# Expert tiles of a mixture-of-experts layer: 32x32 block transposes on VectorE placed by DMA, in place of transposes on TensorE, with the down products two tiles behind

## The chip, the cores and the metric

One core of one Trainium2 chip runs the whole program. The metric is the device time in microseconds (us) of one execution. TensorE (PE in the profile) does matmuls and transposes, VectorE (DVE), ScalarE (ACT) and GpSimd (POOL) elementwise work; SyncE (SP) and ScalarE issue the plain DMAs here, GpSimd the indirect ones.

## The reference

Four residual steps on x, 4 x 512 tokens of 512 dims: a cross-attention that yields softmax weights, a ternary Hadamard feed-forward, a grouped cross-attention with 32 heads, and a routed mixture of experts. Only the last is touched by the change:

```python
def _routed_moe(x, gate_w, w0, w1, wo):          # x: 2048 x 512, E = 8 experts, K = 2, M = 1024
    logits = jnp.einsum('td,de->te', x, gate_w)
    top_logits, top_idx = jax.lax.top_k(logits, K)
    top_w = jax.nn.softmax(top_logits, axis=-1)
    cw = jnp.zeros((T, E), dtype=x.dtype).at[jnp.arange(T)[:, None], top_idx].add(top_w)
    out = jnp.zeros_like(x)
    for e in range(E):
        h = jax.nn.silu(x @ w0[e]) * (x @ w1[e])
        out = out + cw[:, e:e + 1] * (h @ wo[e])
    return out
x = x + moe(layernorm(x))
```

## The kernel before

The stages before the experts take about 920 us and are not touched. They end with a scatter: each normed token is written, with its weight beside it, to two rows of `sorted_x` in DRAM, one for each of its experts, so that every expert's rows lie together. An expert's rows are cut into tiles of 128. How many tiles an expert has is known only at run time; the table `plan` in SBUF holds for each tile its rows in `sorted_x`, the place of its result, the weights' columns and its expert. The program always runs 39 tiles (`MTILES`), enough for every split; those past the last used one are empty and are worked like the others.

**One tile** (`step`). ScalarE's queue loads 128 rows (`sorted_tokens`, two buffers). TensorE transposes them (`transpose_x`, 4 transposes into bank 4), ScalarE rounds the result to its first part (`x_first`), VectorE makes the remainder (`x_second`). fp32 products are made from such pairs of parts: `products` does three matmuls of 512 columns (first x first, first x second, second x first). Gate and up are done in two halves of 512 inner columns, each 2 x 4 x 3 = 24 matmuls, each into two banks. ScalarE takes Silu of the gate bank into `expert_inner`, VectorE multiplies it by the up bank. TensorE then transposes `expert_inner` (8 transposes, L2999), and ScalarE and VectorE split it in two parts (L1560, L2246). The down products (`down`, 8 x 3 matmuls into bank 7) follow; VectorE scales the result by the row's weight (`move_y`), and ScalarE's queue stores it to `sorted_y`.

**Order on TensorE in step i**: gate and up of tile i, the transposes of the tokens of tile i+1, the down products of tile i-1, the transposes of the inner rows of tile i. So one tile's down products are run one step behind its gate and up. Each engine runs its instructions in the order in which they are written, in a loop of two steps for tiles 3 to 36, with the first three and last two written out.

**The weights.** SyncE loads each expert's gate and up weights (2 x 2 MB, `load_w_in`) into one of two places, by the expert's parity, once the gates of the expert two before are done, and the down weights (2 MB, `load_wo`) into a single place. GpSimd splits them into two parts: a cast and a subtraction for each quarter or half, L1075 and L1076 (`half_split`). TensorE waits for the first and the second half of gate and up by `w_in_parts`, and for the two halves of the down weights by `wo_parts`. GpSimd's order is written by hand, and no line of it is in the diff:

```python
for e in range(1, EXPERTS):
    w_in_split(e, 0)
    w_in_split(e, 1)
    end = pool.value_load(row8_i["wait"][0:1, e - 1:e], min_val=1, max_val=MTILES + 1)
    pool.wait_ge(e_wo, end)      # the down products of all tiles up to expert e-1 are done
    pool.sem_inc(pool_waited, 1)
    wo_split(e)
```

`w_in_split(e, h)` does the half h of both weights (two pairs of cast and subtraction), `wo_split(e)` two pairs, the first for k = 0 to 3 of the down products.

**The end.** When all used tiles are stored, GpSimd gathers each token's two rows from `sorted_y` and adds them to x (32 indirect DMAs, L1058), and SyncE writes the output as they land (L803). The empty tiles run meanwhile.

## Time and profile before

| what | value |
|---|---|
| time, median of 3 runs | 1641.98 us (1639.44 to 1642.45) |
| the profiled execution | 1643.14 us, its span 1641.3 us |
| mean granted TensorE clock | 0.985 of full speed |
| TensorE busy | 1565.4 us, 95% of the span |
| VectorE busy | 938.9 us, 57% |
| ScalarE busy | 717.1 us, 44% |
| GpSimd busy | 702.1 us, 43% |
| chain that ended last | PE 78%, DVE 13%, ACT 3%, issue 3%, POOL 2%, DMA 1% |

Busy time counts the work of an engine, not its waits or its issuing of DMAs. The span is from the first to the last instruction of one profiled execution, and the time of that execution lies some 1.8 us above its span. The share of an engine is a mean over the whole kernel; the expert stage is the last 720 us of it. In the timelines, `SPq` and `ACTq` are the DMA issues of SyncE and ScalarE, a bracket gives the idle time before an instruction and the work that ended it, and `xN` merges N instructions.

### The profile page before, as it was taken

The numbers are of one execution on the slowest core, as the hardware profiler recorded it, in microseconds if no ns is written. First come the engines' busy times: TensorE is split into PE (matmuls) and PEld (weight loads), VectorE is DVE, ScalarE is ACT, GpSimd is POOL, SyncE is SP. The second block draws the span as 40 slices with busy tenths as digits, with TensorE's granted clock in tenths as the row PEclk, the third lists the DMA queues.
The fourth block names the chain that finished last, engine by engine and source line by source line (L and its number), as shares of the span: only waits on it lengthen the run. The fifth ranks groups of instructions, "written<-read, shape, count | busy, mean of one in ns | idle before, by whom it ended". The sixth has DMA issues, their size and how long they took to land.

```text
span 1641.3 us, 24692 instructions
## 1 busy us (share of the span) xinstructions
PE 1565.4 (95%) x8277; PEld 1046.3 (64%) x8278; DVE 938.9 (57%) x1540; ACT 717.1 (44%) x1166; POOL 702.1 (43%) x479
## 2 busy tenths in 40 slices
PE   6879999999999999999998799999999999999998
PEld 4565757575753333434333788888888888888886
DVE  6898979797888898988884622222222222222221
ACT  5885646464537777777676211111111111111111
POOL 2224352534513125353464756651781270930074
PEclk9889999999999999999999999999999999999999
DMA  9189800000331445353431642323421323510088
GB/s 355 51 306 386 323 1 1 1 1 1 101 80 49 134 125 155 91 146 102 146 104 61 211 155 95 132 77 137 179 77 34 133 77 128 180 39 26 32 142 211
DMA packets 90945, 196.18 MB, mean 120 GB/s; under 512 B 7153, under 2 KB 9074, under 8 KB 90226
## 3 DMA queue, kind: packets, MB, share of 16 engines
q1 hardware_dynamic: 71746, 156.68, 28.5%
q0 software_dynamic: 7168, 17.04, 4.6%
q10 hardware_dynamic: 11952, 21.43, 3.9%
q8 instruction: 46, 0.75, 0.2%
q14 instruction: 33, 0.27, 0.1%
HBM read 113.28 MB, written 81.32 MB: 119 GB/s over the span
## 4 chain that ended last, share of the span: by engine, by line
PE 78%; DVE 13%; ACT 3%; issue 3%; POOL 2%; DMA 1%; another core or an unknown queue 0%; SPq 0%; DVEq 0%; POOLq 0%; ACTq 0%
PE psum L2976 13%; PE psum L2978 13%; PE psum L2977 13%; PE psum L2619 7%; PE psum L2830 6%; PE psum L2819 5%; PE psum L2634 5%; DVE neg_max L2094 4%; PE psum L2793 3%; PE psum L2664 3%; PE psum L2999 2%; DMA x_tiles<-in_x 1%; PE psum L2954 1%; DVE ternary_rows L1697 1%; PE psum L2809 1%
## 5 line engine op out<-in xcount | busy, mean ns | idle before, releaser
L2094 DVE TENSOR_REDUCE neg_max<-psum 128x2 f32<-128x1024 f32 x248 | 291.9, 1220 | 44.1 <-PE psum L2793 42.0
L1450 ACT ACTIVATE probabilities<-psum 128x512 f32<-128x512 f32 x512 | 270.3, 603 | 82.2 <-PE psum L2819 78.1
L2236 DVE TENSOR_TENSOR expert_inner<-psum,expert_inner 128x512 f32<-128x512 f32 x78 | 53.9, 692 | 382.6 <-ACT expert_inner L1555 377.5
L2976 PE MATMUL psum<-expert_weight_parts,sorted_tokens_t_first 128*128 x624 | 249.7, 400 | 4.9 <-issue 3.1
L2978 PE MATMUL psum<-expert_weight_parts,sorted_tokens_t_second 128*128 x624 | 246.3, 395 | 0.0
L2977 PE MATMUL psum<-expert_weight_parts,sorted_tokens_t_first 128*128 x624 | 246.2, 395 | 0.0
L1555 ACT ACTIVATE expert_inner<-psum 128x512 f32<-128x512 f32 x78 | 46.7, 599 | 390.2 <-PE psum L2978 390.2
L2819 PE MATMUL psum<-query_rows,key_rows 50*128 50x512 f32 x512 | 181.4, 445 | 5.1 <-ACT probabilities L1450 1.7
L2793 PE MATMUL psum<-key_rows,query_rows 48*128 48x512 f32 x496 | 173.0, 480 | 6.0 <-DVE neg_max L2094 3.3
L2830 PE MATMUL psum<-probabilities,value_and_one 128*32 128x512 f32 x1024 | 139.8, 619 | 1.5 <-ACT probabilities L1450 0.9
L2976 PEld LDWEIGHTS psum<-expert_weight_parts,sorted_tokens_t_first 128*128 128x128 f32 x624 | 117.3, 188 | 32.4 <-issue 5.9
L2819 PEld LDWEIGHTS psum<-query_rows,key_rows 50*128 50x128 f32 x512 | 78.3, 187 | 90.0 <-issue 37.7
L2978 PEld LDWEIGHTS psum<-expert_weight_parts,sorted_tokens_t_second 128*128 128x128 f32 x624 | 117.4, 188 | 27.3
L2977 PEld LDWEIGHTS psum<-expert_weight_parts,sorted_tokens_t_first 128*128 128x128 f32 x624 | 117.4, 188 | 26.2
L1075 POOL CAST expert_weight_parts<-wo_of_expert 128x2048 fp32r<-128x2048 f32 x16 | 30.4, 1897 | 241.5 <-PE psum L2978 241.5
L1560 ACT ACTIVATE expert_inner_t_first<-psum 128x512 fp32r<-128x512 f32 x78 | 42.6, 596 | 202.0 <-PE psum L2999 202.0
L2976 PE MATMUL psum<-expert_weight_parts,expert_inner_t_first 128*128 128x512 f32 x312 | 125.9, 403 | 1.6 <-DVE expert_inner_t_second L2246 1.6
L2978 PE MATMUL psum<-expert_weight_parts,expert_inner_t_second 128*128 128x512 f32 x312 | 122.2, 392 | 0.0
L2977 PE MATMUL psum<-expert_weight_parts,expert_inner_t_first 128*128 128x512 f32 x312 | 122.1, 391 | 0.0
L2263 DVE TENSOR_SCALAR expert_out<-psum,row_weight 128x512 f32<-128x512 f32 x39 | 29.3, 750 | 161.0 <-PE psum L2978 156.9
L866 POOL TENSOR_TENSOR inner_half_rotated_t<-inner_t 128x512 f32<-128x512 f32 x56 | 75.4, 1367 | 80.0 <-DVE inner_t L1935 79.7
L1028 POOL TENSOR_TENSOR x_tiles<-x_tiles,attended_normed 128x256 f32<-128x256 f32 x31 | 22.7, 733 | 202.2 <-DVE attended_normed L2141 202.2
(317 smaller groups left out, 2966.0 us busy)
## 6 DMA issues: line engine op xcount, KB each, us to landing
sorted_x<-zero_rows SPq DMA_DIRECT2D x9, 3960.0 KB, 30.5
w_of_odd_expert<-in_L_ffn_w SPq DMA_DIRECT2D x8, 2048.0 KB
wo_of_expert<-in_L_ffn_wo SPq DMA_DIRECT2D x7, 2048.0 KB, 8.5
query_rows<-query_rows_of_units SPq DMA_DIRECT2D x64, 192.0 KB, 3.5
w_of_even_expert<-in_L_ffn_w SPq DMA_DIRECT2D x6, 2048.0 KB, 10.7
sorted_tokens<-sorted_x ACTq DMA_DIRECT2D x39, 264.0 KB, 2.7
sorted_y<-expert_out ACTq DMA_DIRECT2D x39, 256.0 KB, 2.1
query_rows_of_units<-dims_first SPq DMA_DIRECT2D x32, 256.0 KB
```

What stands on the lines that cost most here:

```text
L866: nc.gpsimd.tensor_tensor(Z[:, chunk_of(r, h) * SEQ:(chunk_of(r, h) + 1) * SEQ], y[0], y[1], op).then_inc(b_half, 1)
L1450: nc.scalar.activation(prob[t % 2][:, i * SEQ:(i + 1) * SEQ], ring(("score", n)), ACT.Exp, scale=HD ** -0.5).then_inc(c_e, 1)
L2094: nc.vector.tensor_reduce(of_pair[:, p, st, :], ring(("max", (m, i))).rearrange("p (h n) -> p h n", h=2), AX.X, ALU.max, negate=True).then ...
L2236: nc.vector.tensor_tensor(h, bank[2 * half + 1], h, ALU.mult).then_inc(e_h, 1)
L2619: last = nc.tensor.matmul(bank[4 + 2 * w + h], wgu_t[w][:, k * FF + f * P:k * FF + (f + 1) * P], q_t[:, k * SEQ:(k + 1) * SEQ], start=(k = ...
L2634: last = nc.tensor.matmul(bank[4 + g], y[:, at:at + P], had[:, k * D:(k + 1) * D], start=(k + part == 0), stop=(k + part == DC))
L2793: done = nc.tensor.matmul(ring(job)[:, h * SEQ:(h + 1) * SEQ], q_r[m % 4][rows, p * SEQ + st * P:p * SEQ + (st + 1) * P], k_r[m % 4][rows, ...
L2819: nc.tensor.matmul(ring(("score", n)), k_r[u % 4][rows, t * P:(t + 1) * P], q_r[u % 4][rows, p * SEQ:(p + 1) * SEQ], start=True, stop=True ...
L2830: last = nc.tensor.matmul(bank[7][32 * h:32 * h + 32, :], v_u[u % KVH][:, t * 32:(t + 1) * 32], prob[t % 2][:, h * SEQ:(h + 1) * SEQ], sta ...
L2976: nc.tensor.matmul(out_bank, hi[:, cols], w_r[:, bass.ds(w_at, 512)], start=start, stop=False)
L2977: nc.tensor.matmul(out_bank, hi[:, cols], w_r[:, bass.ds(w_at + BLOCK, 512)], start=False, stop=False)
L2978: return nc.tensor.matmul(out_bank, lo[:, cols], w_r[:, bass.ds(w_at, 512)], start=False, stop=stop)
```

## The change

Both kinds of transposes in the expert stage leave TensorE. VectorE transposes 32x32 blocks in place (`blocks`), from SBUF into the same PSUM banks as before, and the DMA that brings the rows puts the blocks where they belong: each of four DMAs fills 32 partitions with runs of 512 bytes (`by_dims`). The 128 dims of a stationary chunk come out in another order than before, so the rows of w0, w1 and wo are handed to the program in that order (`laid_out`, a permutation of rows). The inner rows lie in SBUF across all partitions, so they are first written to DRAM (`keep`) and brought back by four DMAs (`bring_back`). Since that takes time, the down products of a tile run two steps behind its gate and up. Token rows have one buffer, the row weight has a DMA of its own (`load_row_weight`). The expert weights are loaded in blocks of 256 columns: 4 DMAs for each gate or up weight, 2 for each down weight.

```diff
@@ -315,15 +315,17 @@
-        x_in = [small.tile(f"sorted_tokens{i}", [P, WIDE]) for i in range(2)]
+        x_in = small.tile("sorted_tokens", [P, D])
...
+        h_in = small.tile("expert_inner_by_dims", [P, MOE])
...
+        inner_d = nc.dram_tensor("expert_inner_rows", (2, 2, P, 512), F32, kind="Internal").ap()
@@ -766,12 +768,14 @@
-                sp.dma_start(w_in_raw[e % 2][i][:].rearrange("p (k m) -> p k m", k=DC),
-                             (w0, w1)[i][e, :, :].rearrange("(k p) m -> p k m", p=P)).then_inc(ld_w[e % 2], 16)
+                for m in range(0, MOE, 256):
+                    sp.dma_start(w_in_raw[e % 2][i][:].rearrange("p (k m) -> p k m", k=DC)[:, :, m:m + 256],
+                                 (w0, w1)[i][e, :, m:m + 256].rearrange("(k p) m -> p k m", p=P)).then_inc(ld_w[e % 2], 16)
...
-                sp.dma_start(wo_raw[:].rearrange("p (k m) -> p k m", k=MOE // P),
-                             wo[e, :, :].rearrange("(k p) m -> p k m", p=P)).then_inc(ld_wo, 16)
+                for m in range(0, D, 256):
+                    sp.dma_start(wo_raw[:].rearrange("p (k m) -> p k m", k=MOE // P)[:, :, m:m + 256],
+                                 wo[e, :, m:m + 256].rearrange("(k p) m -> p k m", p=P)).then_inc(ld_wo, 16)
@@ -1532,43 +1536,79 @@
-                def load(i, parity):
-                    act.wait_ge(e_xtr, i + 1)
-                    if not (static(i) and i < 2):
-                        act.wait_ge(e_xw, i - 1)
-                    nc.scalar.dma_start(x_in[parity][:], sorted_x[bass.ds(row_of(i), P), :]).then_inc(e_ld[parity], 16)
+                def by_dims(to, rows, done):
+
+                    for a in range(4):
+                        nc.scalar.dma_start(to[32 * a:32 * a + 32].rearrange("r (b c) -> r b c", c=P),
+                                            rows[:, a * P:(a + 1) * P].rearrange("(b r) c -> r b c", r=32)).then_inc(done, 16)
+
+                def load(i):
+                    if not static(i) or i > 0:
+                        act.wait_ge(e_xtr, i)
+                    by_dims(x_in, sorted_x[bass.ds(row_of(i), P), 0:D], e_ld)
+
+                def load_row_weight(i, parity):
+                    if not static(i) or i > 0:
+                        act.wait_ge(e_xw, 16 * i)
+                    if not static(i) or i > 1:
+                        act.wait_ge(e_y, i)
+                    nc.scalar.dma_start(row_w[parity][:], sorted_x[bass.ds(row_of(i), P), D:WIDE]).then_inc(e_xw, 16)
+
+                def keep(i, parity):
+                    act.wait_ge(e_h, 2 * i + 4)
+                    nc.scalar.dma_start(inner_d[parity].rearrange("h t c -> t h c"),
+                                        h_d[:].rearrange("t (h c) -> t h c", h=2)).then_inc(e_kept, 16)
+
+                def bring_back(i, parity):
+                    act.wait_ge(e_kept, 16 * i + 16)
+                    if not static(i) or i > 0:
+                        act.wait_ge(e_htr, 2 * i)
+                    by_dims(h_in, inner_d[parity].rearrange("h t c -> (h t) c"), ld_had)
+
+                def inner_first(i):
+                    act.wait_ge(e_wo, i + 1)
+                    for half in range(2):
+                        act.wait_ge(e_htr, 2 * i + half + 1)
+                        nc.scalar.activation(h_hi_d[:, half * 512:(half + 1) * 512], bank[5 + half], ACT.Copy).then_inc(e_hh, 1)
...
                 def x_first(i):
-                    act.wait_ge(e_xtr, 2 + i + 1)
+                    act.wait_ge(e_xtr, i + 1)
+                    act.wait_ge(e_gu, 1 + 2 * i)
                     nc.scalar.activation(x_hi[:], bank[4], ACT.Copy).then_inc(e_xh, 1)
...
                 def step(i, parity):
-                    if not static(i) or i + 2 < MTILES:
-                        load(i + 2, parity)
+                    if not static(i) or i > 1:
+                        inner_first(i - 2)
+                    if not static(i) or i > 2:
+                        store(i - 3, 1 - parity)
+                    if not static(i) or i > 0:
+                        load_row_weight(i - 1, 1 - parity)
                     for half in range(2):
                         act.wait_ge(e_gu, 1 + 2 * i + half + 1)
-                        act.wait_ge(e_htr, 2 * i + half + 1)
                         nc.scalar.activation(h_d[:, half * 512:(half + 1) * 512], bank[2 * half], ACT.Silu).then_inc(e_silu, 1)
...
                         x_first(i + 1)
-                    for half in range(2):
-                        act.wait_ge(e_htr, 2 + 2 * i + half + 1)
-                        nc.scalar.activation(h_hi_d[:, half * 512:(half + 1) * 512], bank[5 + half], ACT.Copy).then_inc(e_hh, 1)
-                    if not static(i) or i > 0:
-                        store(i - 1, 1 - parity)
-
+                    keep(i, parity)
+                    if not static(i) or i + 2 < MTILES:
+                        load(i + 2)
+                    bring_back(i, parity)
...
                 act.wait_ge(*scattered(3))
-                load(0, 0)
-                load(1, 1)
+                load(0)
                 x_first(0)
+                load(1)
                 tile_loop(act, step)
+                inner_first(MTILES - 2)
+                store(MTILES - 3, 0)
+                load_row_weight(MTILES - 1, 0)
+                inner_first(MTILES - 1)
+                store(MTILES - 2, 1)
                 store(MTILES - 1, 0)
@@ -2230,26 +2270,43 @@
                 def step(i, parity):
+                    if not static(i) or i > 1:
+                        inner_second(i - 2)
                     for half in range(2):
...
                     if not static(i) or i + 1 < MTILES:
+                        x_transposed(i + 1)
                         x_second(i + 1)
                     if not static(i) or i > 0:
-                        move_y(i - 1, 1 - parity)
-                    if not static(i) or i + 1 < MTILES:
-                        row_weight(i + 1, 1 - parity)
+                        inner_transposed(i - 1)
+                    if not static(i) or i > 1:
+                        move_y(i - 2, parity)
+
+                def inner_transposed(i):
+                    if not static(i) or i > 0:
+                        dve.wait_ge(e_hl, 2 * i)
+                    dve.wait_ge(ld_had, 64 * i + 16 + 64)
+                    for half in range(2):
+                        blocks(bank[5 + half], h_in[:, half * 512:(half + 1) * 512]).then_inc(e_htr, 1)
+
+                def inner_second(i):
                     for half in range(2):
...
-                def row_weight(i, parity):
-                    if not (static(i) and i < 2):
-                        dve.wait_ge(e_y, i)
-                    dve.wait_ge(e_ld[parity], 8 * (i - parity) + 16)
-                    nc.vector.tensor_copy(row_w[parity][:], x_in[parity][:, D:D + 1]).then_inc(e_xw, 1)
+                def x_transposed(i):
+                    if not static(i) or i > 0:
+                        dve.wait_ge(e_xl, i)
+                    dve.wait_ge(e_ld, 64 * i + 64)
+                    blocks(bank[4], x_in[:]).then_inc(e_xtr, 1)
+
+                def blocks(to, rows):
+
+                    return nc.vector.transpose(to.rearrange("p (k b r) -> p b k r", k=4, b=4),
+                                               rows.rearrange("p (b k j) -> p b k j", b=4, k=4))
@@ -2257,14 +2314,19 @@
                     dve.wait_ge(e_wo, i + 2)
+                    dve.wait_ge(e_xw, 16 * i + 16)
                     if not (static(i) and i < 2):
...
+                x_transposed(0)
                 x_second(0)
-                row_weight(0, 0)
                 tile_loop(dve, step)
+                inner_second(MTILES - 2)
+                inner_transposed(MTILES - 1)
+                move_y(MTILES - 2, 1)
+                inner_second(MTILES - 1)
                 move_y(MTILES - 1, 0)
@@ -2947,13 +3009,6 @@
-                def transpose_x(i, parity):
-
-                    pe.wait_ge(e_ld[parity], 8 * (i - parity) + 16)
-                    for k in range(DC):
-                        last = nc.tensor.transpose(bank[4][:, k * P:(k + 1) * P], x_in[parity][:, k * P:(k + 1) * P], ident[:])
-                    last.then_inc(e_xtr, 1)
-
@@ -2989,26 +3044,16 @@
                         last.then_inc(e_gu, 1)
-                    if not static(i) or i + 1 < MTILES:
-                        transpose_x(i + 1, 1 - parity)
-                    if not static(i) or i > 0:
-                        down(i - 1)
-                    for half in range(2):
-                        pe.wait_ge(e_h, 2 * i + half + 3)
-                        for k in range(4):
-                            last = nc.tensor.transpose(bank[5 + half][:, k * P:(k + 1) * P],
-                                                       h_d[:, (4 * half + k) * P:(4 * half + k + 1) * P], ident[:])
-                        last.then_inc(e_htr, 1)
+                    if not static(i) or i > 1:
+                        down(i - 2)
                 pe.wait_ge(d_plan, 1)
-                transpose_x(0, 0)
                 tile_loop(pe, step)
+                down(MTILES - 2)
                 down(MTILES - 1)
-            pe.sem_inc(e_xtr, 2)
             pe.sem_inc(e_gu, 1)
             pe.sem_inc(e_wo, 1)
-            pe.sem_inc(e_htr, 2)
             phase_a()
@@ -3037,6 +3082,16 @@
+def laid_out(name, a):
+
+
+    if name not in ("L1_ffn_w0", "L1_ffn_w1", "L1_ffn_wo"):
+        return a
+    experts, rows, columns = a.shape
+    a = a.reshape(experts, rows // 512, 4, 4, 32, columns).swapaxes(2, 3)
+    return np.ascontiguousarray(a.reshape(experts, rows, columns))
+
+
```

## Rows read from the trace of the kernel before

**Rows 1.** The view of busy time by window, inside the expert stage, all engines.
```profile
1200.00:1400.00 200.00, 200.00 (x934) 164.17 (x933) 45.49 (x77) 30.87 (x56) 79.77 (x26) 1.00 0.27 93
```

**Rows 2.** The timeline of one expert tile: start, length, engine, line, operation.
```profile
1206.87 0.60 PE L2954 MATMUL psum<-ident,sorted_tokens 128*128 128x128 f32 x4
1207.07 0.60 ACT L1555 ACTIVATE expert_inner<-psum 128x512 f32<-128x512 f32 x1 [4.89 <-PE psum L2978]
...
1207.54 0.39 PE L2977 MATMUL psum<-expert_weight_parts,expert_inner_t_first 128*128 128x512 f32 x1
...
1207.70 0.69 DVE L2236 TENSOR_TENSOR expert_inner<-psum,expert_inner 128x512 f32<-128x512 f32 x1 [4.80 <-ACT expert_inner L1555]
...
1208.31 0.68 DVE L2256 TENSOR_TENSOR sorted_tokens_t_second<-psum,sorted_tokens_t_first 128x512 fp32r<-128x512 f32 x1
...
1212.57 0.40 PE L2978 MATMUL psum<-expert_weight_parts,expert_inner_t_second 128*128 128x512 f32 x1
...
1212.80 1.04 PE L2999 MATMUL psum<-ident,expert_inner 128*128 128x128 f32 x8
...
1213.91 0.39 PE L2977 MATMUL psum<-expert_weight_parts,sorted_tokens_t_first 128*128 x1
```

**Rows 3.** The timeline of SyncE's DMA queue in the expert stage.
```profile
972.85 2.18 SPq L769 DMA_DIRECT2D w_of_even_expert<-in_L_ffn_w  x2
...
1026.90 0.92 SPq L769 DMA_DIRECT2D w_of_odd_expert<-in_L_ffn_w  x2
...
1116.95 0.92 SPq L769 DMA_DIRECT2D w_of_even_expert<-in_L_ffn_w  x2
...
1171.01 0.92 SPq L769 DMA_DIRECT2D w_of_odd_expert<-in_L_ffn_w  x2
...
1279.14 0.92 SPq L769 DMA_DIRECT2D w_of_even_expert<-in_L_ffn_w  x2
...
1369.15 0.92 SPq L769 DMA_DIRECT2D w_of_odd_expert<-in_L_ffn_w  x2
...
1423.21 0.37 SPq L800 DMA_DIRECT2D x_tiles_again<-out  x1
1598.76 31.66 SPq L803 DMA_DIRECT2D out<-x_tiles_again  x16
```

**Rows 4.** The timeline of GpSimd; in brackets its idle time and releaser.
```profile
997.02 1.90 POOL L1075 CAST expert_weight_parts<-wo_of_expert 128x2048 fp32r<-128x2048 f32 x1 [30.41 <-PE psum L2978]
...
1032.28 4.62 POOL L1076 TENSOR_TENSOR expert_weight_parts<-w_of_even_expert,expert_weight_parts 128x2048 fp32r<-128x2048 f32 x1 [0.18 <-POOL expert_weight_parts L1075]
...
1559.86 1.65 POOL L1058 DMA_INDIRECT x_tiles_again<-sorted_y,slot_of_result  x1 [99.11 <-DMA sorted_y<-expert_out]
```

**Rows 5.** The timeline of ScalarE around the last store that GpSimd awaits.
```profile
1556.88 0.36 ACTq L1543 DMA_DIRECT2D sorted_y<-expert_out  x1
```

**Rows 6.** The timeline of the first tile's start.
```profile
923.01 1.45 ACTq L1539 DMA_DIRECT2D sorted_tokens<-sorted_x  x2
...
927.23 0.69 DVE L2256 TENSOR_TENSOR sorted_tokens_t_second<-psum,sorted_tokens_t_first 128x512 fp32r<-128x512 f32 x1 [0.40 <-ACT sorted_tokens_t_first L1547]
...
928.31 0.49 PE L2976 MATMUL psum<-expert_weight_parts,sorted_tokens_t_first 128*128 x1 [1.75 <-DVE sorted_tokens_t_second L2256]
```

**Rows 7.** The DMA view: KB each, median us from issue to landing.
```profile
sorted_y<-expert_out ACTq DMA_DIRECT2D x39, 256.0 KB, 2.1
...
context_of_first_batch<-in_ctx SPq DMA_DIRECT2D x1, 256.0 KB, 2.8
```

**Rows 8.** Windows of TensorE: length, busy us (count), granted clock, DMA share, GB/s.
```profile
47.00:50.80 3.80, 0.45 (x5) 0.68 0.00 0
50.80:57.50 6.70, 6.70 (x23) 0.50 0.00 0
918.80:922.00 3.20, 0.21 (x1) 1.00 0.47 186
922.00:925.80 3.80, 3.80 (x19) 0.55 0.36 81
```

More of the change, by code:

```diff
@@ L317, in network @@
         small.at = first_small + 32 * 1024
-        x_in = [small.tile(f"sorted_tokens{i}", [P, WIDE]) for i in range(2)]
+        x_in = small.tile("sorted_tokens", [P, D])
         x_hi = small.tile("sorted_tokens_t_first", [P, D], F32R)
         x_lo = small.tile("sorted_tokens_t_second", [P, D], F32R)
-        row_w = [small.tile(f"row_weight{i}", [P, 1]) for i in range(2)]
+        row_w = [small.tile(f"row_weight{i}", [P, WIDE - D]) for i in range(2)]
         y_out = [small.tile(f"expert_out{i}", [P, D]) for i in range(2)]
         h_d = small.tile("expert_inner", [P, MOE])
+        h_in = small.tile("expert_inner_by_dims", [P, MOE])
         h_hi_d = small.tile("expert_inner_t_first", [P, MOE], F32R)
@@ L355, in network @@
         w_out = [sem("w_out_even"), sem("w_out_odd")]
-        ld_had, had_ready = sem("ld_had"), sem("had_ready")
+        ld_had, had_ready = sem("ld_had_then_inner_back"), sem("had_ready")
         b_normed, b_trans, b_trans_sb, b_fw, b_fac = sem("b_normed"), sem("b_trans"), sem("b_trans_sb"), sem("b_fw"), sem("b_fac")
@@ L383, in network @@
         d_sc, d_zf = [sem("d_sc_even"), sem("d_sc_odd")], sem("d_zf")
-        e_ld, e_st = [sem("e_ld0"), sem("e_ld1")], [sem("e_st0"), sem("e_st1")]
+        e_ld, e_kept, e_st = sem("e_ld"), sem("e_kept"), [sem("e_st0"), sem("e_st1")]
         e_xtr, e_xh, e_xl, e_gu, e_silu, e_h, e_htr, e_hh, e_hl, e_wo, e_y = (
@@ L593, in w_in_loaded @@
         def w_in_loaded(e):
-            return ld_w[e % 2], 32 * (e // 2 + 1) + (96 if e % 2 == 0 else 0)
+            return ld_w[e % 2], 128 * (e // 2 + 1)
         def wo_loaded(e):
-            return ld_wo, 16 * (e + 1) + 48
+            return ld_wo, 64 + 32 * e
         def by_tile(a, e=EXPERTS):
@@ L784, in _ @@
             sp.wait_ge(*scattered(3))
-            sp.wait_ge(e_ld[1], 16)
+            sp.wait_ge(e_ld, 64)
             load_w_in(1, 1)
@@ L3046 @@
     for name, a in [(n, inputs[n]) for n in _INS] + list(constants().items()):
-        a = np.ascontiguousarray(a)
+        a = laid_out(name, np.ascontiguousarray(a))
         arrays[f"in_{name}"] = a
```

## The prediction, made before the change was built

> **What bounds the kernel now.** I read the view of windows first. The expert stage runs from about 928 us to the end, and inside it TensorE is busy in 200.00 of 200.00 us at full clock, while GpSimd is busy in 79.77, VectorE in 45.49 and ScalarE in 30.87 [rows 1]. So a product or a transpose taken away there is worth its whole time, as long as nothing else becomes late. Second, the timeline of one tile, to price what is taken away [rows 2]. Third, SyncE's and GpSimd's timelines, because they tell how many tiles each expert has and how long the weights take to be ready [rows 3, 4]. Fourth, what sets the end: GpSimd's gathers follow the last used tile's store [rows 4, 5], and the output rows follow them [rows 3].
>
> SyncE issues the weights of expert e when the gates of expert e-2 are done. 1026.90 to 1116.95 is 90.05 us, which is 5 tiles of 18.01; the seven rows give 3, 5, 3, 6, 5 and 3 tiles to experts 1 to 6 [rows 3]. Expert 0 has 3, since 928.31 [rows 6] to 972.85 [rows 3] is 44.5 us, two steps and a gate part. Experts 0 to 6 hold 28 tiles; the gathers start 1559.86 [rows 4], which leaves expert 7 tiles 28 to 33. Tiles 34 to 38 are empty but run too. I write S(i) for the start of step i and f for an expert's first tile.
>
> **Part 1: twelve transposes leave TensorE.** Down products start every (1212.57 - 1207.54)/22 = 0.229 us [rows 2]. Four transposes of the tokens and one product take 1207.54 - 1206.87 = 0.67, so the four cost 0.44. Eight of the inner rows and one product take 1213.91 - 1212.80 = 1.11, so the eight cost 0.88 [rows 2]. A step loses 1.32 us: 18.01 becomes 16.7, of which down is 24 x 0.229 = 5.5 and gate/up 11.2. Over 39 steps that is 51.5 us, if TensorE stays fed.
>
> **Part 2: block transposes on VectorE.** The trace has none on VectorE. Bounds for one of 128x512 (T): VectorE's passes over PSUM of that size take 0.68 and 0.69 [rows 2], and twice that is the upper bound (1.4), half of it the lower (0.35). I take 0.7, the nearest row. What matters is the chain into the next tile. It starts at the end of gate/up, 1206.87: Silu at +0.20, 0.60 long; its multiplication from 1207.70 to +1.52 [rows 2]; now the transpose T, the first part 0.6, the second part 0.68, and 0.3 to 0.4 until TensorE starts (927.23 + 0.69 to 928.31 [rows 6]). That is 3.9 us with T = 0.7. Down of 5.5 us covers it, up to T = 2.3. Three transposes a tile add 2.1 us to a VectorE that is idle for three quarters. The Trainium skill speaks against moving them: "VectorE: DVE Perf Modes", Rules for kernel authors, gives a full 128x128 transpose to TensorE when PSUM is where it goes. Its section on the three transpose paths has 311 ns for 128x128 of 16-bit data on VectorE; four of those would be an estimated T of 1.24, and by it the sum below would be about 1 us more. No run here shows it yet.
>
> Steps 0 and 1 have no down product as cover, so TensorE stands for 3.9 us twice. Now step 0 has a similar but shorter chain.
>
> **Part 3: the DMA work of ScalarE.** Per tile there were 2 issues, now 11: 4 for tokens, 1 row weights, 1 keep, 4 back, 1 store. An issue is 0.35, and two with a plan value read between them take 1.45, so the read adds 0.75 [rows 6]. That is 11 x 0.35 + 3 x 0.75 = 6.1 us; with five passes of 0.6 and a wait for keep to land (2.1, the nearest row being a store of half its size [rows 7]) 11.2 of 16.7. Behind the wait for keep stand the four issues back, the first parts of the tile before and its store. In order: keep at about S + 14.2, tokens until S + 16.7, back until S(i+1) + 1.5, first parts until 2.7, store at 3.5 to 4.5 (I take 4.0), before Silu wants the engine at 5.8. VectorE takes the rows at S(i+1) + 14.9: 256 KB in 512-byte runs land in 2.8 us [rows 7], so twice that size in 2.8 to 5.6, against 13 to spare. Hidden. If the issues cost more, see rival 1.
>
> **Part 4: down two tiles behind.** This is what GpSimd feels. It prepares weights in a fixed order: down weights of e once the last down product of e-1 is done, then the gate and up weights of e+1. With down one tile behind, the former starts at S(f+1), where f is e's first tile; now at S(f+2). Its six pairs end 1032.28 + 4.62 - 997.02 = 39.9 us later [rows 4]. The last of them are needed for the second half of gate/up of e+1. For expert 1, now: that is 1026.9 + 0.44 + 5.5 + 0.88 + 5.6 = 1039.3 [rows 3], and they are ready at 1036.9 [rows 4], 2.4 us before. GpSimd starts about 0.5 us into a step (997.02 [rows 4] against 972.85 + 0.44 + 5.5 + 0.88 + 11.2 + 0.44 + 5.5 = 996.8). With the change the parts are ready 0.5 + 39.9 = 40.4 after S(f+2), and needed at (n-2) x 16.7 + 5.6: for n = 3 tiles at 22.3, so TensorE stands 18.1 us; for n = 5 or 6 not at all (55.7). Three experts whose successor must be prepared have 3 tiles: 1, 3 and 6. Expert 0 escapes, as its down weights wait for no product. 3 x 18.1 = 54.3 us: more than part 1 gives. The second half of the down weights is ready 0.5 + 13.3 = 13.8 after S(f+2) and needed at 11.2 + 12 x 0.229 = 13.9: no wait, at worst 0.2 us seven times.
>
> A standing TensorE also falls to half clock. After 3.2 us with 0.21 busy the next 3.80 were granted 0.55, which costs 1.7; after 3.80 with 0.45 busy 6.70 were granted 0.50, which costs 3.4 or more [rows 8]. I take 1.8 for each of five restarts that count (two without cover, three experts), and up to 5 for the range.
>
> **Part 5: weights in column blocks.** 8 issues of 1 KB runs for gate and up in place of 2, 2 in place of 1 for down. They are issued about 46 us before GpSimd needs them. Nothing on the path; the bounds are 0 and a microsecond at the first tile.
>
> **The sum.** First product: the tokens now need four issues (+1.3) and T in place of 0.44: 928.3 + 1.5 = 929.8. S(1) = +15.1 = 944.9. S(2) = +15.1 + 1.8 = 961.8. S(3) = +16.7 + 1.8 = 980.3. S(36) = 980.3 + 33 x 16.7 + 3 x (18.1 + 1.8) = 1591.1. Tile 33's down products end there, its store is issued at +4.0 = 1595.1. Now it is issued at 1556.88 [rows 5]: 38.2 later. What follows is a chain of its own: gathers and output rows, whose last issue ends 1598.76 + 31.66 = 1630.4 and lands 2.1 later, 1632.5 [rows 3, 7]. Now it is hidden behind the empty tiles; with 38.2 added it ends at 1670.7. TensorE's own end: S(36) + 2 x 16.7 + 11.2 + 3 x 5.5 + two waits for the inner rows of about 2.5 + 3.5 for the last store = about 1661, so it is 10 us short of deciding. So the gathers, one step later behind the moved down products, set the end. The span is 1641.30 in an execution of 1643.14, so the time is 1672.5 beside that; the median of the runs is 1.16 lower, so I forecast 1671.
>
> **The rivals.** (1) ScalarE's queue becomes the bound. For it: 11 issues, and a wait on a DMA with everything queued behind. If each issue costs the 1.1 us of an issue with its plan read [rows 6], the engine needs 11 x 1.1 + 3.0 + 2.8 = 17.9 us a tile, 1.2 more than TensorE; over the 33 steps to S(36) that is 40: 1711. Against it: the issues back need no plan value. It decides from 1.0 us an issue. The Trainium skill, "DMA: Bandwidth & Descriptors", Bandwidth, calls transfers under 64 KB dominated by their descriptors; the parts here are 64 and 128 KB, at its edge, and the nearest row is the 2.8 us. (2) The other side: the weights are ready in time after all, because the order on GpSimd or the tile counts are other than I read. Then 3 x (18.1 + 1.8) = 59.7 us go, and 1671 becomes 1611. The wait decides below four tiles (at four it is 40.4 - 33.4 - 5.6 = 1.4). Against it stand the spacings of 54 us in [rows 3]. (3) The pieces cancel: that takes stands near 8 us in place of 18, 1671 - 30 = 1641. Nothing speaks for that size.
>
> **Chances.** Forecast 0.80, its own range 1657 to 1690 (no clock loss -9; 5 us each +16). Rival 1 0.10, rival 2 0.08, rival 3 0.02. Range 1655 to 1695. A difference under 0.2% can't be told from none here; faster 0.08, within 0.2% 0.02, slower 0.90.
>
> **What would show it.** Step starts 16.7 us apart; TensorE idle about 10 us before and 6 to 8 us inside the first gate/up of experts 2, 4 and 7 (tiles 6, 14, 28), released by GpSimd's weight parts; GpSimd's idle before the down weights about as long as now or gone in those; a VectorE transpose near 0.7; the gathers starting near 1598. Wrong if a transpose takes over 2.3 us, if TensorE waits for the token parts in every tile, if steps are longer than 17, or if the wait at tile 6 is missing.

## The result, and the profile after

The changed kernel takes 1679.97 us (median of 4 runs, 1677.15 to 1682.73) against 1642.22 us (4 runs, 1639.44 to 1648.20): 1.022 of the time before, 95% interval 1.020 to 1.025. It is slower by 2.2%; the forecast was 1671 in 1655 to 1695. Its profiled execution took 1680.92 us.

The page of the changed kernel: the span, busy time, and the chain that ended last.

```profile
span 1679.1 us, 24925 instructions
...
PE 1535.0 (91%) x7809; PEld 1011.8 (60%) x7810; DVE 1011.2 (60%) x1618; ACT 720.9 (43%) x1166; POOL 699.8 (42%) x479
...
PE 68%; DVE 13%; POOL 9%; ACT 3%; issue 3%; DMA 1%; ACTq 0%; another core or an unknown queue 0%; POOLq 0%; SPq 0%; DVEq 0%
```

TensorE is busy 30 us less than before and the span is 38 us longer. In the chain GpSimd has 9%, where it had 2. The view of who waited for whom, TensorE from 936 us on (total, times, longest):

```profile
PE psum L3031 <- POOL expert_weight_parts L1080: 46.6, 7, 10.2
PE psum L3031 <- DVE expert_inner_t_second L2298: 10.3, 2, 8.2
PE psum L3031 <- DVE sorted_tokens_t_second L2313: 9.8, 3, 3.5
```

Seven waits for GpSimd's weight parts, 46.6 us; of the three for the tokens' second parts, 3.5, 3.5 and 2.8, the last is ahead of the very first product. Before, TensorE waited for no weight part in that view, and in 1200 to 1400 us for nothing at all [rows 1]. The pair at the first tile of expert 2 (tile 6):

```profile
1044.86 0.79 PE L3031 MATMUL psum<-expert_weight_parts,sorted_tokens_t_first 128*128 x1 [10.17 <-POOL expert_weight_parts L1080]
...
1057.87 0.79 PE L3031 MATMUL psum<-expert_weight_parts,sorted_tokens_t_first 128*128 x1 [5.62 <-POOL expert_weight_parts L1080]
```

10.17 us before its first half, 5.62 inside it. The same pair, 10.2 and 5.6, then 10.2 and 4.7, stands at tiles 14 and 28, the first tiles of experts 4 and 7. GpSimd's timeline there, and its first gather:

```profile
1018.23 1.90 POOL L1079 CAST expert_weight_parts<-wo_of_expert 128x2048 fp32r<-128x2048 f32 x1 [45.21 <-PE psum L3033]
...
1040.13 4.49 POOL L1080 TENSOR_TENSOR expert_weight_parts<-w_of_even_expert,expert_weight_parts 128x2048 fp32r<-128x2048 f32 x1 [0.18 <-POOL expert_weight_parts L1079]
...
1053.23 4.49 POOL L1080 TENSOR_TENSOR expert_weight_parts<-w_of_even_expert,expert_weight_parts 128x2048 fp32r<-128x2048 f32 x1 [0.18 <-POOL expert_weight_parts L1079]
...
1601.86 1.65 POOL L1062 DMA_INDIRECT x_tiles_again<-sorted_y,slot_of_result  x1 [92.14 <-DMA sorted_y<-expert_out]
```

The down weights of expert 1 start at 1018.23; in [rows 4] that work began one tile earlier in the sequence. The two halves of expert 2's weights are ready at 1040.13 + 4.49 = 1044.62 and 1053.23 + 4.49 = 1057.72, and TensorE goes on 0.2 us behind each. The windows over this stand (length, busy, granted clock, DMA share, GB/s):

```profile
1038.00:1048.40 10.40, 3.54 (x8) 0.51 1.12 327
1048.40:1055.30 6.90, 3.85 (x17) 0.99 1.10 348
1055.30:1062.10 6.80, 4.23 (x10) 0.51 0.12 38
```

The granted clock fell to half during each wait and stayed there after the products went on, as in [rows 8]: 3.54 and 4.23 us of busy time in the first and the third window ran at half clock, which costs 1.8 and 2.1 us. What one stand (TensorE idle, and the half clock with it) costs in all can be read from the spacing of ScalarE's Silu of the second half, tile 5 to tile 6; and there is a second kind of long step, whose first product is in the last row below:

```profile
1028.89 0.60 ACT L1592 ACTIVATE expert_inner<-psum 128x512 f32<-128x512 f32 x1 [4.85 <-PE psum L3033]
...
1065.58 0.60 ACT L1592 ACTIVATE expert_inner<-psum 128x512 f32<-128x512 f32 x1 [12.70 <-PE psum L3033]
...
1105.21 0.49 PE L3031 MATMUL psum<-expert_weight_parts,sorted_tokens_t_first 128*128 x1 [0.89 <-issue]
```

1065.58 - 1028.89 = 36.69, where a step without a stand takes 16.49 (below): 20.2 us for this stand, and the same way 20.3 and 21.1 for those at tiles 14 and 28. At 1105.21, three tiles behind an expert's first, TensorE idles 0.89 us with no wait that the profile shows; four such steps are 1.1 to 1.6 us longer than 16.49, 5.5 together. VectorE's transposes (shortest, median, longest, in ns):

```profile
L2308 DVE STREAM_TRANSPOSE psum<-expert_inner_by_dims x78: 682/702/729, 968.0 to 1659.7; 128x512 f32<-128x512 f32 x78
L2308 DVE STREAM_TRANSPOSE psum<-sorted_tokens x39: 714/717/718, 933.4 to 1624.8; 128x512 f32<-128x512 f32 x39
```

ScalarE and its queue: the inner rows going back in a tile without a weight load in flight, and then a tile from its Silu of the second half (1132.89) to the same of the next, with a load in flight:

```profile
1121.84 1.83 ACTq L1542 DMA_DIRECT2D expert_inner_by_dims<-expert_inner_rows  x4
...
1132.89 0.60 ACT L1592 ACTIVATE expert_inner<-psum 128x512 f32<-128x512 f32 x1 [4.85 <-PE psum L3033]
...
1135.06 0.39 ACTq L1559 DMA_DIRECT2D expert_inner_rows<-expert_inner  x1
...
1142.96 1.84 ACTq L1542 DMA_DIRECT2D expert_inner_by_dims<-expert_inner_rows  x4
1145.33 1.09 ACT L1572 ACTIVATE expert_inner_t_first<-psum 128x512 fp32r<-128x512 f32 x2 [9.76 <-issue]
...
1149.38 0.60 ACT L1592 ACTIVATE expert_inner<-psum 128x512 f32<-128x512 f32 x1 [0.73 <-PE psum L3033]
```

A DMA issue takes 1.83 / 4 = 0.46 us, and a step without a stand 1149.38 - 1132.89 = 16.49. The write of the inner rows, issued at 1135.06, lets them go back only at 1142.96, and what is queued behind waits with them. Last, SyncE's queue: the loads that follow the gates of tiles 10 and 19, and the output rows.

```profile
1132.89 10.31 SPq L772 DMA_DIRECT2D w_of_even_expert<-in_L_ffn_w  x8
...
1303.15 9.23 SPq L772 DMA_DIRECT2D w_of_even_expert<-in_L_ffn_w  x8
...
1641.57 34.89 SPq L807 DMA_DIRECT2D out<-x_tiles_again  x16
```

The gathers begin at 1601.86 and the last output row is issued at 1641.57 + 34.89 = 1676.46, 2.6 us before the end.

In the profiled execution the expert stage starts 7.3 us later (935.61 against 928.31 [rows 6]). I expected 1.5. Of the 7.3, 6.7 are there already at GpSimd's last scatter ahead of the stage (925.89 against 919.23), so only 0.6 belong to the chain of the first tile. The 6.7 lie in code that is the same in both kernels, but for the form of the first weight loads, and these do not order the starts: that scatter comes at 924.1 with whole loads in `before37` and at 918.8 with column blocks in `early3`. Ahead of it TensorE's granted clock was 0.84 from 484 to 528 us (0.96 before) and 0.88 from 704 to 748 us (0.96 before), and equal or within 0.02 in all other windows of 44 us; over the profiled executions of all kernels here the first product starts anywhere from 924.8 to 935.6, and at 935.2 for the kernel before with 37 tiles. That the clock accounts for all of it is not shown. So I compare stages from the first product to the end: 713.0 before, 743.5 after, 740.9 by my sum.

### The profile page after: what moved, and what is told of

Same layout as the page of the kernel before. It is cut to its first block, busy times and chain, and to the rows that moved or that the text cites. A ratio compares the mean times of both kernels' runs of the same rounds, so it can differ in the third digit from the quotient of the medians.

```text
span 1679.1 us, 24925 instructions
## 1 busy us (share of the span) xinstructions
PE 1535.0 (91%) x7809; PEld 1011.8 (60%) x7810; DVE 1011.2 (60%) x1618; ACT 720.9 (43%) x1166; POOL 699.8 (42%) x479
## 3 DMA queue, kind: packets, MB, share of 16 engines
q10 hardware_dynamic: 87456, 62.34, 12.6%
## 4 chain that ended last, share of the span: by engine, by line
PE 68%; DVE 13%; POOL 9%; ACT 3%; issue 3%; DMA 1%; ACTq 0%; another core or an unknown queue 0%; POOLq 0%; SPq 0%; DVEq 0%
PE psum L3031 11%; PE psum L3032 11%; PE psum L3033 11%; PE psum L2681 7%; PE psum L2892 5%; POOL expert_weight_parts L1080 5%; PE psum L2881 5%; DVE neg_max L2134 5%; PE psum L2696 5%; PE psum L2855 3%; PE psum L2726 3%; POOL expert_weight_parts L1079 2%; DVE ternary_rows L1737 1%; PE psum L2871 1%; ACT inner_quantised_t L1360 1%
## 5 line engine op out<-in xcount | busy, mean ns | idle before, releaser
L1592 ACT ACTIVATE expert_inner<-psum 128x512 f32<-128x512 f32 x78 | 46.6, 598 | 321.1 <-PE psum L3033 285.9
L3031 PEld LDWEIGHTS psum<-expert_weight_parts,sorted_tokens_t_first 128*128 128x128 f32 x624 | 121.1, 194 | 90.5 <-issue 64.7
L3032 PEld LDWEIGHTS psum<-expert_weight_parts,sorted_tokens_t_first 128*128 128x128 f32 x624 | 121.2, 194 | 25.6
L3033 PEld LDWEIGHTS psum<-expert_weight_parts,sorted_tokens_t_second 128*128 128x128 f32 x624 | 121.0, 194 | 26.0
L2298 DVE TENSOR_TENSOR expert_inner_t_second<-psum,expert_inner_t_first 128x512 fp32r<-128x512 f32 x78 | 50.3, 686 | 102.8 <-ACT expert_inner_t_first L1572 102.8
```

The source lines that it names most:

```text
L3031: nc.tensor.matmul(out_bank, hi[:, cols], w_r[:, bass.ds(w_at, 512)], start=start, stop=False)
L3032: nc.tensor.matmul(out_bank, hi[:, cols], w_r[:, bass.ds(w_at + BLOCK, 512)], start=False, stop=False)
L3033: return nc.tensor.matmul(out_bank, lo[:, cols], w_r[:, bass.ds(w_at, 512)], start=False, stop=stop)
```

## The experiments

Two groups of four and one of two; kernels of a group ran on the same chip, beside the kernel before. Its median was 1646.89 beside the first group, 1641.43 beside the second and 1647.03 beside the third, so ratios are compared.

**GpSimd's order: `early3_sp` and `early2`.** In the changed kernel, part of the next expert's gate and up weights is split ahead of the present expert's down weights: three of its four pairs in `early3_sp` (shown), two in `early2`.

```diff
-                for e in range(1, EXPERTS):
-                    w_in_split(e, 0)
-                    w_in_split(e, 1)
+                w_in_split(1, 0)
+                w_in_split(1, 1)
+                for e in range(1, EXPERTS):
+                    if e + 1 < EXPERTS:
+                        for j in range(3):
+                            w_in_pair(e + 1, j)
...
                     wo_split(e)
+                    if e + 1 < EXPERTS:
+                        for j in range(3, 4):
+                            w_in_pair(e + 1, j)
```

In `early3_sp` SyncE also issues the gate and up weights of expert e+1 before the down weights of e:

```diff
-                    sp.wait_ge(wo_parts, 2 * e)
-                    load_wo(e)
+                if e > 2:
+                    sp.wait_ge(wo_parts, 2 * (e - 1))
+                    load_wo(e - 1)
```

> The changed kernel with GpSimd's order changed: three of the four pairs of the next expert's gate and up weights are split before the down weights of the present one, the fourth after them; SyncE issues the next expert's gate and up weights ahead of the present one's down weights. If GpSimd's order costs the three stands of 19.9 us, as my theory has it, they go: 1680 - 60 = 1620, with 5 more where weights land late, 1616 to 1630, faster than the kernel before. If ScalarE's queue or the round trip through DRAM bound the steps (rival 1), nothing changes: 1680.

> The changed kernel with two of the four pairs (the first half of gate and up) split before the down weights, SyncE's order as in the changed kernel. By my theory the second half is ready 0.5 + 13.3 + 13.3 = 27.1 after S(f+2) and needed at 22, so each of the three stands shrinks from 19.9 to about 5 to 7: 1680 - 3 x 14 = 1638 (1630 to 1645). A theory in which the stand is another wait that only shows at GpSimd gives 1680.

Measured: `early3_sp` 1621.02 us, 0.985 of before (0.982 to 0.988); `early2` 1639.64, 0.9955 (0.9931 to 0.9979). Both are as the theory of GpSimd's order had them, and 40 to 60 us off what the rival theories had (1680). TensorE's waits in `early3_sp`:

```profile
PE psum L3042 <- DVE expert_inner_t_second L2309: 10.1, 2, 8.1
...
PE psum L3042 <- POOL expert_weight_parts L1091: 5.2, 4, 2.5
```

46.6 us of waits for GpSimd became 5.2 in `early3_sp`. In `early2`, where SyncE is as in the changed kernel and only GpSimd's order differs, they became 11.7 in 3 waits.

**What sets the end: `after37` and `before37`.** Both kernels with two empty tiles less, which leaves out work only other splits of the tokens would need.

```diff
-MTILES = 2 * TILES + EXPERTS - 1
+MTILES = 2 * TILES + EXPERTS - 3
```

> The changed kernel with 37 tiles in place of 39: two empty tiles less, which only other splits of the tokens would need. If the gathers and output rows set the end, as my sum has it, two tiles of 16.5 us less on TensorE change nothing or little: 1680, at most 3 less from less DMA traffic. If TensorE sets the end, 1680 - 33 = 1647.

> The kernel before with 37 tiles in place of 39. There TensorE's end lies 9 us behind that of the gathers by my reading, so of the 36 us taken from TensorE only about 9 come back: 1633. If the gathers don't matter, 1606.

Measured: `after37` 1675.73, 1.018 (1.014 to 1.023), against 1.022 with 39 tiles; `before37` 1639.88, 0.995 (0.993 to 0.997), which is 7 us. From the first product to the end, `after37` takes 739.6 (743.5 with 39) and `before37` 704.3 (713.0): 3.9 and 8.7 us less, where TensorE does 33 and 36 us less. So the gathers and output rows set the end after; before, TensorE set it, and they were done some 9 us ahead of it. The 3.9 us are a little over the 3 that I allowed, and come from faster gathers, as the next rows show. The output rows in SyncE's queue of `after37`:

```profile
1640.36 31.03 SPq L807 DMA_DIRECT2D out<-x_tiles_again  x16
```

The gathers start at 1601.76 there, so from the first gather to the last output issue it is 69.6 us in `after37`, 74.6 with 39 tiles, and 70.6 before [rows 3, 4]. The gathers thus run some 4 us slower beside the tiles of the changed kernel, whose ScalarE queue moves 62.34 MB in place of 21.43. The other kernels order themselves the same way: the same stretch takes 70.1 to 71.1 us where ScalarE's queue is as before (`before37`, `before_early3`), 72.7 in `tokens_only`, 74.5 to 76.8 in the five other variants with 39 tiles and one round trip of the inner rows, and 78.3 in `keep_twice`, which writes them twice.

**One part alone: `tokens_only`.** The kernel before, with only the tokens' transposes moved to VectorE; inner rows over TensorE, down one tile behind, GpSimd and loads untouched. The rows of the gate and up weights are laid out to suit, as in the changed kernel.

```diff
+                    by_dims(x_in, sorted_x[bass.ds(row_of(i), P), 0:D], e_ld)
...
+                    blocks(bank[4], x_in[:]).then_inc(e_xtr, 1)
...
-                    if not static(i) or i + 1 < MTILES:
-                        transpose_x(i + 1, 1 - parity)
```

> One part alone: the kernel before, with only the transposes of the tokens moved to VectorE and their rows brought in blocks by four DMAs; inner rows still go over TensorE, down one tile behind, weights in whole loads. A step loses 0.44 us (18.0 to 17.6), 39 of them 17 us; step 1 starts about 2 later. GpSimd's weights stay 1 us ahead even for experts with 3 tiles (ready 40.4, needed 17.6 x 2 + 5.6 = 40.8). By my theory 1646.9 - 14 = 1633 on this chip, faster by 0.9%. If VectorE's transposes or the block loads cost a step anything, no gain: 1647 or more.

Measured: 1621.15, 0.987 (0.985 to 0.990): 20 us faster, where 14 were expected. Silu of the second half, two tiles apart, on ScalarE:

```profile
1301.95 0.60 ACT L1567 ACTIVATE expert_inner<-psum 128x512 f32<-128x512 f32 x1 [4.76 <-PE psum L2990]
...
1336.91 0.60 ACT L1567 ACTIVATE expert_inner<-psum 128x512 f32<-128x512 f32 x1 [4.76 <-PE psum L2990]
```

(1336.91 - 1301.95) / 2 = 17.48 a step (17.47 in the mean of 34 steps): 0.54 less than 18.01, not 0.44. TensorE waits for no weight part.

**SyncE's order: `early3`.** GpSimd as in `early3_sp`, SyncE as in the changed kernel.

> As the kernel with three pairs ahead of the down weights, but SyncE in its old order (down weights of the present expert ahead of the next expert's gate and up weights). By my theory the weights of experts 3 and 5 land 3 to 5 us later behind an expert with 3 tiles, so the down weights behind them are late: 1621 + 4 to 9 = 1628. If SyncE's order is nothing: 1621.

Measured: 1640.66, 0.9995 (0.998 to 1.001). SyncE's order is worth 1.4% or some 24 us, where I gave it 4 to 9: the direction held, the size did not. GpSimd's order alone brings 1.022 to 0.9995, SyncE's the rest of the way to 0.985. TensorE's waits for GpSimd:

```profile
PE psum L3042 <- POOL expert_weight_parts L1091: 23.6, 8, 7.7
```

The loads in SyncE's queue and the first cast of expert 3's weights on GpSimd, in `early3`:

```profile
1026.91 0.99 SPq L777 DMA_DIRECT2D wo_of_expert<-in_L_ffn_wo  x2
1028.52 15.56 SPq L772 DMA_DIRECT2D w_of_odd_expert<-in_L_ffn_w  x8
```

```profile
1054.94 1.90 POOL L1090 CAST expert_weight_parts<-w_of_odd_expert 128x2048 fp32r<-128x2048 f32 x1 [21.40 <-DMA w_of_odd_expert<-in_L_ffn_w]
```

and in `early3_sp`:

```profile
1024.27 9.68 SPq L772 DMA_DIRECT2D w_of_odd_expert<-in_L_ffn_w  x8
1033.99 5.35 SPq L777 DMA_DIRECT2D wo_of_expert<-in_L_ffn_wo  x2
```

```profile
1043.90 1.90 POOL L1090 CAST expert_weight_parts<-w_of_odd_expert 128x2048 fp32r<-128x2048 f32 x1 [7.78 <-DMA w_of_odd_expert<-in_L_ffn_w]
```

The stage itself starts 2.5 us earlier in `early3` (first product at 928.52, against 931.07). Counted from there, the eight issues start 6.8 us later behind the down weights and take 15.56 in place of 9.68 us, and the weights are there 13.6 us later. The down weights' load has to wait for its single place: it is issued at 1026.91, right when GpSimd has split the down weights that lay there (1026.89), and holds back what is behind it in the queue. Since the order now puts the next expert's weights ahead of the down weights on GpSimd, the down weights are late, by 7.66 and 1.00 at the first down products of expert 2 and 6.83 and 1.59 at those of expert 4.

**Part 5 undone: `after_whole` and `early3_sp_whole`.** Expert weights loaded in whole DMAs, as before the change.

```diff
-                for m in range(0, MOE, 256):
-                    sp.dma_start(w_in_raw[e % 2][i][:].rearrange("p (k m) -> p k m", k=DC)[:, :, m:m + 256],
-                                 (w0, w1)[i][e, :, m:m + 256].rearrange("(k p) m -> p k m", p=P)).then_inc(ld_w[e % 2], 16)
+                sp.dma_start(w_in_raw[e % 2][i][:].rearrange("p (k m) -> p k m", k=DC),
+                             (w0, w1)[i][e, :, :].rearrange("(k p) m -> p k m", p=P)).then_inc(ld_w[e % 2], 16)
```

> The changed kernel with the expert weights loaded as before, one DMA for each weight with runs of 4 KB and 2 KB, in place of column blocks of 1 KB runs. My theory has this part at nothing: 1680, within 3. If column blocks keep the round trip of the inner rows short while weights are in flight, the round trip gets longer than the 5 us to spare and the steps under a load stretch: 1685 to 1700. If their small runs delay the weights, it is faster than 1677.

> Three pairs ahead of the down weights and SyncE reordered (0.985 of the kernel before), and the expert weights in whole loads as before the change. The whole loads made the changed kernel some 5 us faster. If they act through earlier landing of the weights, the 5 us that TensorE still waits for GpSimd here shrink: 0.981 to 0.984 of the kernel before. If column blocks did what they were for, by keeping the round trip of the inner rows short, this is slower than 0.985.

Measured: 1.019 (1.016 to 1.022) against 1.022 (1.020 to 1.025), and 0.983 (0.981 to 0.985; 1617.73 us) against 0.985 (0.982 to 0.988). In both pairs the intervals overlap, so column blocks are at best no gain; if anything they cost a few us. TensorE's two longest entries of waiting in `early3_sp_whole` (it has none for GpSimd):

```profile
PE psum L3040 <- DVE expert_inner_t_second L2307: 8.8, 2, 6.7
PE psum L3040 <- DVE sorted_tokens_t_second L2322: 7.0, 2, 3.5
```

Of all kernels run this one is the fastest, 1.7% faster than before.

**ScalarE's queue: `keep_twice`.** `early3_sp` with every tile's inner rows written twice, both writes awaited.

```diff
-                    nc.scalar.dma_start(inner_d[parity]..., h_d...).then_inc(e_kept, 16)
+                    for copy in range(2):
+                        nc.scalar.dma_start(inner_d[parity + 2 * copy]..., h_d...).then_inc(e_kept, 16)
...
-                    act.wait_ge(e_kept, 16 * i + 16)
+                    act.wait_ge(e_kept, 32 * i + 32)
```

> The fastest kernel so far (three pairs ahead, SyncE reordered, 1621) with every tile's inner rows written to DRAM twice, and both writes awaited: one issue more on ScalarE's queue and a longer wait in each of 39 tiles. If ScalarE's queue has slack (my theory), at most 5 us slower, from steps under a weight load, where the write already takes 8 us. If it is at its limit (rival 1), each step grows by 1 to 2 us: 1660 to 1700.

Measured: 1631.61, 0.992 (0.990 to 0.994): 0.7% or 11 us slower than `early3_sp`, between the two expectations, so more than the 5 us that my theory allowed. From expert 2's load to that of the output tiles it took 433.0 us (971.13 to 1404.09) against 426.5 in `early3_sp`, 6.5 us over 25 tiles or 0.26 a tile. The rest is at the end: TensorE's waits for the inner rows grew from 10.1 to 20.5 us, the longest from 8.1 to 12.6, and its last product starts at 1625.40, when the last output row is already issued (1588.76 + 36.29 = 1625.05), so here it is TensorE's end that decides. The queue of `keep_twice` under a weight load: the two writes, and the rows going back.

```profile
1112.08 0.99 ACTq L1571 DMA_DIRECT2D expert_inner_rows<-expert_inner  x2
...
1122.02 1.86 ACTq L1553 DMA_DIRECT2D expert_inner_by_dims<-expert_inner_rows  x4
```

9.9 us from the writes to the rows' return, against 7.9 above. So one write, as in the changed kernel, does not bind a usual step, and a second one begins to.

**GpSimd's order in the kernel before: `before_early3`.**

> The kernel before with GpSimd's order of the fastest version (three pairs of the next expert's weights ahead of the down weights), and nothing else. With down one tile behind, the down weights are wanted at S(f+1), some 18 us after the first tile's start, but the next expert's weights land at about S(f) + 10 to 14 and take 20 more, so the down weights start 12 to 16 late for experts 1 to 6: 1642 + 6 x 12 = 1714 (1690 to 1740). If the order were simply the better one, 1642 or less.

Measured: 1697.90, 1.033 (1.028 to 1.037), some 50 us slower, in the range, but near its lower end: some 50 us over six experts are 8.5 for each, where I had 12. TensorE's waits:

```profile
PE psum L2987 <- POOL expert_weight_parts L1087: 37.7, 12, 7.1
```

The order that makes the changed kernel fast makes the one before slow. What the right order is depends on how far behind the down products run.

## Why the prediction held, point by point

**Part 1** was right in kind and a sixth too small. A step without a stand takes 16.49 us, not 16.7. `tokens_only` shows that four transposes are worth 0.54, and the eight then about 1.0. What I missed is in the gate and up products, 47 of them from the second one on: before, up to the tokens' transposes behind them,

```profile
1213.91 0.39 PE L2977 MATMUL psum<-expert_weight_parts,sorted_tokens_t_first 128*128 x1
...
1224.87 0.60 PE L2954 MATMUL psum<-ident,sorted_tokens 128*128 128x128 f32 x4
```

and after, up to the first down product:

```profile
1122.02 0.40 PE L3032 MATMUL psum<-expert_weight_parts,sorted_tokens_t_first 128*128 x1
...
1132.69 0.40 PE L3031 MATMUL psum<-expert_weight_parts,expert_inner_t_first 128*128 128x512 f32 x1
```

10.96 us before and 10.67 after, so 0.3 less for the same products; in `tokens_only` it is 10.70 already (1308.43 to 1319.13). I had priced the transposes by their own rows alone. Why the products run closer together stays open.

**Part 2**: T is 0.70 and 0.72 us, as taken. The two steps without cover stood 3.5 us each, not 3.9. In no other step did TensorE wait for the tokens. The estimate of 1.24 from the Trainium skill, "VectorE: DVE Perf Modes", The three transpose paths, is above what was measured. The advice of the Trainium skill, "VectorE: DVE Perf Modes", Rules for kernel authors, to leave a 128x128 transpose to TensorE when PSUM is where it goes, does not hold in this case for the tokens: `tokens_only` is 1.3% faster.

**Part 3**: 0.46 us an issue in the eight block issues of a tile (0.37 to 0.39 in the other three) where I took 0.35, still under the 1.0 from which it would decide. The write of the inner rows takes up to 8 us under a weight load, where I took 2.1. That was hidden, with 2 us left: in the tile shown above VectorE has the inner rows' second parts done 1.9 us after the start of the first parts at 1145.33, which is 1147.25, and the down products are due at about 1149.2. Rival 1 is out, but not by as much as the sum said.

**Part 4** carried the result. Each stand was put at 18.1 + 1.8 = 19.9 us and took 20.2, 20.3 and 21.1. What the sum lacked is the second kind of long step: the loads at 1132.89 and 1303.15 are 9 steps and one stand apart, and 170.26 - 9 x 16.49 = 21.9 is the stand of 20.3 and one such step's 1.6. Three stands at experts with 3 tiles, none at those with 5 or 6, as worked out; `early3_sp` and `early2` show the cause, and `before_early3` the other way round. Rivals 2 and 3 are out.

**Part 5** was put at nothing, and nothing it is, within what the runs can tell.

**The sum**: from S(3) to S(36) I had 610.8 us (1591.1 - 980.3), and in the rows of TensorE it is 611.2:

```profile
984.82 0.39 PE L3031 MATMUL psum<-expert_weight_parts,sorted_tokens_t_first 128*128 x1
...
1596.02 0.39 PE L3031 MATMUL psum<-expert_weight_parts,sorted_tokens_t_first 128*128 x1
```

That it is so close is luck in part: 33 shorter steps took 6.9 us away, the stands added 1.9 and the four long steps that I had not foreseen 5.5. The gathers start 38.2 us later, I said; it was 42.0. The first product is 5.8 us later than I had it: the 6.7 ahead of the stage were not in my sum, and the chain to the first product grew by 0.6 where I had 1.5. The end by the gathers and not by TensorE was right, and `after37` shows it. What I missed is that the gathers themselves slow down by 4 us, and that TensorE's last two tiles wait 8.2 and 2.1 us for their inner rows, where I had 2.5 and 2.5; this cost nothing, since the gathers end later. From my 1670.7 for the span to 1679.1 it is 8.4 us: 5.8 up to the first product, 2.0 less up to the gathers (666.3 from the first product, where I had 668.3), 4.0 in the gathers, 0.5 behind the last output issue.

**What the change would have needed**: of its parts, the tokens' transposes give 1.3% by themselves. The inner rows add to that only if GpSimd and SyncE prepare the weights in another order, and then by 0.2% (`early3_sp`, 0.982 to 0.988, which overlaps the 0.985 to 0.990 of `tokens_only`) or 0.5% with whole loads (`early3_sp_whole`, 0.9807 to 0.9849 against 0.9852 to 0.9895, just apart).

## What to carry to other kernels

Before a product is moved a tile later, look for what waits on its end: here GpSimd's single place for the down weights, and behind it in a written order the next expert's weights. A margin of 2.4 us in one row became 15 to 16 us of waiting, three times, and with the half clock ate the whole gain of the transposes that left TensorE. Count run-time sized groups one by one: the mean of 34 / 8 = 4.25 tiles an expert would have shown no wait at all. And test the parts alone: moving 4 of the 12 transposes held most of the gain.

## What the hardware showed that I had not expected

- Taking 12 transposes out of a step saved 1.5 us, 0.13 us each, where their own spacing in the timeline made it 0.11; the gate and up products beside them ran 0.3 us shorter in all.
- A 512 KB write from SBUF to DRAM that lands in 2.7 us in the median (from issue to landing, in `after_whole`) let the rows behind it go only 7.9 us after its issue while 4 MB of weights came in on another queue.
- Eight load issues of 512 KB took 9.7 us of SyncE's queue, and 15.6 us right behind two issues of 1 MB, where two issues of 2 MB took 0.9 us [rows 3].
- In code that is the same in all kernels here but for the form of the first weight loads, the last scatter ahead of the expert stage came anywhere from 915.1 (`tokens_only`) to 925.9 us (`after`). From 484 to 528 us the granted clock was 0.96 in the former and 0.84 in the latter.
